# Last expert layer: 56 row picks ahead of the first put in place of 40, and a ring of two dense tiles in place of four

## The reference

```python
def _L0_ffn_ref(x, gate_w, experts):
    ...
    gate_logits = jnp.einsum('bnd,de->bne', x, gate_w)
    competitive_gates = sinkhorn(gate_logits)
    vals, idx = jax.lax.top_k(jnp.swapaxes(competitive_gates, -1, -2), M)
    ...
    routed = x[b_idx, routed_indices]
    ...
    outputs = jnp.einsum('ebmd,edf->ebmf', routed, experts)
    outputs = outputs * jnp.transpose(gate_values, (2, 0, 1))[..., None]
    ...
    routed_back = jnp.zeros_like(x).at[b_idx, routed_indices].set(vals_bmed)
    return routed_back
...
x = x + 0.5 * _L0_ffn_ref(_layernorm(x, axis=-1), L0_ffn_gate_w, L0_ffn_experts)
```

## Time and profile before

| | us |
|---|---|
| median of 3 runs | 3512.19 |
| lowest, highest | 3511.89, 3519.33 |
| profiled execution, its own time | 3510.05 |
| its span in the trace | 3508.4 |
| DVE busy over the span | 3132.1 (89%) |
| PE busy | 2715.5 (77%) |
| ACT busy | 2127.5 (61%) |
| POOL busy | 1311.4 (37%) |

### The profile page before, as it was taken

The page is one execution under the profiler, slowest core; times in us unless marked ns, Lnnn a source line. Parts: engine busy times, 40 slices in busy tenths (PEclk is TensorE's granted clock), DMA queues, the critical chain, the costliest instruction groups (busy, mean ns, idle before and its releaser), DMA issues. The chain is left out here.

```text
span 3508.4 us, 29860 instructions
## 1 busy us (share of the span) xinstructions
PE 2715.5 (77%) x9684; PEld 1495.6 (43%) x9684; DVE 3132.1 (89%) x2608; ACT 2127.5 (61%) x2275; POOL 1311.4 (37%) x871
## 2 busy tenths in 40 slices
PE   7105877899899789988978998898789577874545
PEld 5003433464345346434634543463345255433444
DVE  8995699999999999999999999999999968995555
ACT  6403668776887777777778768777866634222111
POOL 0004372445346344634634372453011010006665
PEclk8556999999999899999999999999999887885778
DMA  6304477789678778867887886788577659233442
GB/s 259 144 1 154 107 160 167 172 167 202 134 169 171 169 169 177 193 142 159 170 182 156 178 188 147 163 171 178 120 148 139 132 117 375 84 144 126 139 141 100
DMA packets 128696, 553.85 MB, mean 158 GB/s; under 512 B 19782, under 2 KB 55272, under 8 KB 79424
## 3 DMA queue, kind: packets, MB, share of 16 engines
q0 software_dynamic: 75168, 393.49, 54.0%
q1 hardware_dynamic: 53408, 158.94, 12.0%
HBM read 137.94 MB, written 117.45 MB: 73 GB/s over the span
## 5 line engine op out<-in xcount | busy, mean ns | idle before, releaser
L1307 DVE TENSOR_TENSOR_SCAN state<-state,drive 128x2048 f32<-128x2048 f32 x512 | 2224.4, 4404 | 53.4 <-ACT state L1513 53.3
L1513 ACT ACTIVATE state<-delta,neg_a 128x2048 f32<-128x2048 f32 x512 | 1019.7, 2005 | 224.2 <-DMA delta<-xc 92.3
L1764 PE MATMUL ps_states<-state,ident 128*128 128x512 f32 x1792 | 846.0, 617 | 86.0 <-DMA state<-state 72.6
L1188 POOL DMA_DIRECT2D state<-state x255 | 234.0, 918 | 1303.4 <-DVE state L1307 1288.3
L1666 PE MATMUL ps_proj<-x1t,w_in 128*128 128x512 f32 x1024 | 502.3, 634 | 88.5 <-ACT xc L1462 30.9
L1764 PEld LDWEIGHTS ps_states<-state,ident 128*128 128x128 f32 x1792 | 345.5, 198 | 484.2 <-issue 379.4
L1682 PE MATMUL ps_proj<-conv_in,tap 128*128 128x512 f32 x1024 | 485.7, 625 | 51.9 <-ACT conv_in L1426 31.0
L1117 POOL DMA_INDIRECT picked<-normed_rows,slot_now x112 | 358.1, 3197 | 95.2 <-PE ps_rows L1647 50.6
L1133 POOL DMA_INDIRECT x<-routed_rows,row_now x112 | 351.5, 3138 | 34.6 <-issue 34.6
L1666 PEld LDWEIGHTS ps_proj<-x1t,w_in 128*128 128x128 f32 x1024 | 202.3, 203 | 366.2 <-issue 265.2
L1682 PEld LDWEIGHTS ps_proj<-conv_in,tap 128*128 128x128 f32 x1024 | 202.8, 201 | 316.4 <-issue 279.3
(11 more groups left out here) (344 smaller groups left out, 3242.2 us busy)
## 6 DMA issues: line engine op xcount, KB each, us to landing
state<-state POOLq DMA_DIRECT2D x255, 1024.0 KB
delta<-xc POOLq DMA_DIRECT2D x24, 1024.0 KB
normed_rows<-kept_rows_in SPq DMA_DIRECT2D x8, 2048.0 KB, 6.3
x_rows<-x SPq DMA_DIRECT2D x16, 1024.0 KB
f_dense<-dense_rows SPq DMA_DIRECT2D x16, 1024.0 KB
kept_rows_in<-in_x SPq DMA_DIRECT2D x7, 2048.0 KB
expert<-in_experts SPq DMA_DIRECT2D x56, 256.0 KB
routed_rows<-routed SPq DMA_DIRECT2D x112, 128.0 KB
```

What stands on the lines that cost most here:

```text
L1188: nc.gpsimd.dma_start(out=state[held(q)][:], in_=state[held(q - 1)][:], accum_op=ALU.add).then_inc(pair_landed(b, q // 2)[0], 16)
L1307: nc.vector.tensor_tensor_scan(state[held(q)][:], state[held(q)][:], drive[j % 2][:], 0.0, ALU.mult, ALU.add).then_inc(state_ready, 1)
L1513: nc.scalar.activation(state[held(q)][:], delta[j % 2][:], ACT.Exp, scale=g.neg_a[:, j, n:n + 1]).then_inc(decay_ready, 1)
L1764: mm = nc.tensor.matmul(ps_sum[c][:], g.ident[:], state[held(q)][:, c * CH:(c + 1) * CH], start=(opening and n == 1), stop=(n == N - 1))
```

## The change

The three constants that size `ffn`'s buffers and order POOL's queue:

```diff
     Q = DENSE * SL
     NR = NB * SL
-    ND, EVERY = 4, 6
-    NX, NI, NO, NB2 = 52, 32, 16, 2
+    ND, EVERY = 2, 6
+    NX, NI, NO, NB2 = 68, 32, 16, 2
     PAIRS = Q // 2
-    AHEAD = 40
+    AHEAD = 56
```

## The result

| | before | changed |
|---|---|---|
| median of 22 runs each, us | 3511.83 | 3517.4 |
| profiled execution, us | 3510.05 | 3517.67 |
| its span, us | 3508.4 | 3516.1 |

The ratio of the changed kernel to the one before is 1.0021, 95% interval 1.0012 to 1.003: 7 us slower, from 4 to 11. The forecast was +2 us and no change that counts; the range of 3495 to 3525 holds the time.

The account below looks back on a forecast made before the run. PE's completion reports, held while POOL issues indirect DMAs back to back, were taken to bound `ffn`, with no engine full. Head +20.0, sixteen slots -18, tiles 0 gave +2 us: forecast 3514, range 3495 to 3525.

Parts of the forecast that it names:

- The mechanism: Head and slot loop of `ffn`: PE's reports crawl while POOL issues indirect DMAs back to back, and catch up once it is quiet.
- The crawl of 0.74 us for each PE instruction: Head: at this pace the 33 instructions up to the last rank matmul need 24 us, supporting the full 20.0 us delay.
- the faster rival: Gap before put 0: reports late for another reason, gap free; put 0 moves 1.3 us, time 3495; chance 0.17.
- Sixteen more picks, +20.0 us: Head: picks ahead of put 0 at 1.253 us each delay POOL's quiet, `f_key`, first finish and put 0 by 20.0 us.
- The loop, saving 18: Loop cut from 72 to 56 pairs: slots 56 to 71 lose their picks, 49.5 us becoming 30.2; 18 us saved.
- The rival (puts alone hold PE too): Slots 56 to 71: puts without picks stay slow; at 2.6 us a slot 7.9 us saved, time 3524; chance 0.26.
- The tail: Last 40 slots, puts alone: 62.9 us before; the sum held no change for it.
- The ring: Dense tiles, two in place of four: loads fit between joins, no tile is waited for; cost zero.
- The range of 3512 to 3522: Whole kernel: the forecast's own range, said to follow from the bounds of the sixteen slots' saving alone.

Follow-up runs that it names:

- e3: Changed kernel with one more wait: POOL stops between pick 39 and pick 40 until DVE's first key step; ratio 0.9984 to the kernel before.
- e10: Kernel before with four short memsets on POOL behind each of the 40 picks ahead of put 0, 2.54 us a pick; one run, 3546.69 us.
- e11: Kernel before with the 112 puts as plain stores on SP's queue, scatter left out, picks still gathers on POOL; one run, 3416.72 us.
- e1: Kernel before with two dense tiles in place of four, still 40 picks ahead and 52 row buffers; ratio 0.9997.
- e2: Kernel before with 24 picks ahead of put 0 in place of 40, 36 row buffers, four dense tiles; ratio 0.9998.
- e4: Kernel before, all sizes kept, with a POOL wait between pick 27 and pick 28 until DVE's first key step; ratio 0.9979.
- e5: Kernel before with 32 picks ahead, 44 row buffers, and a POOL wait for DVE's first key step between pick 23 and pick 24; ratio 0.9991.
- e6: Kernel before with 36 picks ahead, 48 row buffers, and a POOL wait for DVE's first key step between pick 23 and pick 24; ratio 0.9973.
- e8: Kernel before with 24 picks ahead and twenty memsets of 128x1024 on POOL behind pick 23; one run, 3523.8 us.
- e12: Kernel before, all sizes kept, with a POOL wait between pick 23 and pick 24 until DVE's first key step; ratio 0.9991.
- e7: Kernel before with all 112 picks as plain loads on SP's queue, gather left out, POOL issuing only puts; one run, 3389.13 us.
- e9: Kernel before with 44 picks ahead, 56 row buffers, three dense tiles, and a POOL wait for DVE's first key step after pick 23; ratio 0.9985.

## Why the prediction was right, and where it was off

- **The mechanism** (reports held by back-to-back picks, released by quiet): shown. e3 and e10 are the plainest, a stop without fewer picks, and fewer per microsecond without a stop. The crawl of 0.74 us for each PE instruction, which the prediction drew on for its upper end, isn't what happened: in the changed kernel PE had run them all by 3191.7, and the last report still came at 3233.5. The Trainium skill's "SBUF — State Buffer", section "Who interferes with whom", says of contention for SBUF's ports that "PE and ACT never wait on anyone", which spoke for the faster rival. No row here shows a matmul slowed by POOL (at its quickest an apply takes 1.89 us in the loop of before as in e11's), so the rule itself stands; but it doesn't cover the reports, and the conclusion drawn from it, that picks in the gap are free, is refuted by put 0, 21.9 us later. The measurement decides.
- **Sixteen more picks, +20.0 us**: put 0 moved by 98.6 - 76.7 = 21.9. The picks took the 20; the reports came 6.1 us after the last one (3233.47 - 3227.37), where I had taken the 4.2 of before.
- **The loop, saving 18**: this term was 2.8 us too large. From put 0 to put 72 the changed kernel took 3445.67 - 3248.00 = 197.7 us, the one of before 212.85: 15.2 saved. Split at put 56 as the prediction splits it, slots 0 to 55 took 166.7 in place of 163.3 us, where "as before" was forecast, and slots 56 to 71 took 31.0 in place of 49.5, where 30.2 was forecast. The split flatters the second half. In the changed kernel the fifth stop, of 4.11 us, ends just at put 56; in the one of before only four lie ahead of it, and two fall behind. In seven other kernels that pair these slots with picks (e1, e2, e4, e5, e6, e8, e12; not e10, whose finishes are far ahead) the first 56 took 162.8 (e6) to 167.9 us (e8), the next sixteen 45.8 to 48.7, and all 72 took 209.9 to 213.7. So the 163.3 and the 49.5 belong to one trace's place of the stops, and the 18.5 that the sixteen saved hit the forecast's 18 by luck as well. The rival (puts alone hold PE too) had the place right, with four short stops of 2.2 to 3.8 us from put 56 up to put 72, but not the price.
- **The tail** took 63.9 us, 1.0 more than before, which I had at nothing.
- **The ring**: nothing, as said; e1 shows it by itself.
- Sum: 21.9 - 15.2 + 1.0 = +7.8 us (the rows unrounded), forecast +2. The mechanism was right, and three terms were off in the same direction: the release after the picks by 1.9 us, the saving of the loop by 2.8, the tail by 1.0. They carried the result just past the 0.2% that I had called no change: the interval leaves out 1, so the kernel is slower, if by little.
- **The range of 3512 to 3522**, which the prediction gives as the forecast's own, doesn't follow from the bounds beside it: savings of 22 and of 0 give 3510 and 3532. That the 3517.4 lies inside it says little.

## What to carry to other kernels

A gap on the issuing engine isn't free because nothing runs in it: ask what it is waiting for, and whether the work that you put in delays just that. Here the gap was the time in which PE's reports got through, so filling it from the front moved it whole, while cutting the block of picks in two, with a short stop where the ranks are due, gave 0.21% with nothing else changed (e4) and 0.27% with four picks fewer ahead as well (e6); with the stop four picks earlier and the sizes of before (e12) no gain is told from noise, so the place must be found by trial. Where events of a late stage are compared, count them from the stage's own start; the start moved by 12 us between profiles of the same code, more than all but the largest effects of this study (e7, e10, e11).

## What the hardware showed that I had not expected

- PE's completion reports depend on how densely POOL issues indirect DMAs. With one each 1.25 to 1.3 us and no stop they come late: PE's last rank matmul ends at 3191.7 in the changed kernel and the key, which waits for it, starts 42 us later; in e10's loop it is 42 and 63 us. They aren't late at once: in the loop of before POOL starts again at 3261.11, and the report of turn(11), ended at 3267.06, is still seen within 1.2 us, while that of turn(12), ended at 3271.31, is seen 17.5 us later. With one each 2.54 us (e10's head) none is late by over 1 us. With runs of two to ten and stops between them (e7, e11) few are, by up to 6.0 us. Twenty memsets in a row do nothing of the kind (e8).
- It is PE's reports alone. In every trace, each of the loop's applies starts at most 0.22 us behind the last of what it asks for: ACT's copy, DVE's finish, PE's own work before it. ACT's and DVE's reports to PE come at once, in the same stretches in which PE's to them don't.
- The delay lies ahead of the semaphore. The trace records when a semaphore is raised, which the views shown here leave out: in the changed kernel that of the first two turns is raised at 3233.51 and 3233.57, though PE's second turn ended at 3196.2, and ACT's copy starts within 0.02 us of the first. What holds the reports there no run shows, nor whether it is POOL's issuing or the transfers still under way: a stop ends both.
- The reports don't come evenly while they are held: with 24 picks in the same order the key came at 35.8 (e2, e9) or 39 to 44 us (e5, e6, e8, e12).
- The price in this kernel is large. With either half of POOL's DMAs taken elsewhere (e7, e11) the last layer takes 232 or 259 us in place of 351. Both leave out part of the work, so this bounds what could be had and isn't a gain; whether a gather can be had at a slower pace without losing the time to POOL itself stays open, since at 224 DMAs of 1.3 us POOL alone needs 291.
